# Two mixtures of experts in a decoder: finding the slots by matrix products, and moving rows per expert

## The reference

```python
gates = softmax(xt @ wg);  expert_idx = argmax(gates)       # 8 experts, one choice
mask1 = one_hot(expert_idx, E);  locations = cumsum(mask1, axis=0) - 1.0
pos = sum(locations * mask1, axis=1);  keep = pos < C        # C = 256 slots per expert
gate_val = sum(gates * mask1, axis=1) * keep
disp = zeros((E * C, M)).at[slot].add(xt * keep)             # rows into slots
h = relu(disp @ w1 + b1);  eo = h @ w2 + b2                  # 256x256x1024 and back
out = eo.reshape(E * C, M)[slot] * gate_val                  # rows back to tokens
```

## Time and profile before

| | us |
|---|---|
| median of 3 runs | 3053.37 (3043.42 to 3053.48) |
| the profiled execution | 3040.47 |
| its span | 3038.7 |
| `l0f`: norm's first operation to the next stage's | 509.7 to 769.0 |
| `l1f`: the same | 1241.4 to 1476.6 |

### The profile page before, as it was taken

One profiled execution on the slowest core, in us unless ns is written; L12 is line 12 of the kernel. 1 busy time (PEld: TensorE's weight loads), 2 busy tenths in 40 slices (PEclk: granted clock), 3 DMA queues, 4 the chain that ended last, 5 costly groups with the idle time before them and its releaser, 6 DMA issues. The chain is left out here.

```text
span 3038.7 us, 29221 instructions
## 1 busy us (share of the span) xinstructions
PE 2160.4 (71%) x10186; PEld 1346.8 (44%) x10217; DVE 1790.3 (59%) x2564; ACT 1185.1 (39%) x1864; POOL 602.7 (20%) x354
## 2 busy tenths in 40 slices
PE   3788898193599979579274888888589766074694
PEld 2455566182223337457122444444446532062374
DVE  4554455222777755511477989898545656945775
ACT  1334222010266644101135988989332224321240
POOL 2321121404142110010401545544002100000100
PEclk8899799596799999789596999999789878577896
DMA  6562100244555200044210000000210000000001
GB/s 151 87 88 25 53 1 1 90 146 85 93 84 69 29 19 1 18 142 137 54 42 14 1 1 1 1 1 1 78 31 1 32 0 0 0 7 0 19 1 34
DMA packets 104551, 124.06 MB, mean 41 GB/s; under 512 B 15824, under 2 KB 95025, under 8 KB 103382
## 3 DMA queue, kind: packets, MB, share of 16 engines
q1 hardware_dynamic: 80820, 95.99, 14.7%
q10 hardware_dynamic: 18978, 16.37, 1.7%
q0 software_dynamic: 4608, 9.85, 1.4%
HBM read 91.11 MB, written 33.03 MB: 41 GB/s over the span
## 5 line engine op out<-in xcount | busy, mean ns | idle before, releaser
L2747 DVE TENSOR_TENSOR_SCAN l2s_h<-l2s_aw 128x2048 f32<-128x2048 f32 x64 | 283.6, 4431 | 3.6 <-PE l2s_c_ps L2696 3.6
L2704 PE MATMUL l2s_big<-g_xn,g_ident 128*128 128x512 f32 x512 | 265.9, 623 | 11.7 <-ACT g_xn L2780 5.8
L2761 POOL TENSOR_SCALAR l2s_aw<-l2s_aw 128x2048 f32<-128x2048 f32 x64 | 241.2, 3769 | 152.0 <-DVE l2s_aw L2739 147.0
L568 DVE TENSOR_REDUCE l1at_nm<-l1at_s 128x1 f32<-128x512 f32 x256 | 162.2, 685 | 66.9 <-PE l1at_s L418 66.1
L2696 PE MATMUL l2s_c_ps<-g_ident,l2s_h 128*128 128x128 f32 x1024 | 156.2, 288 | 45.3 <-ACT g_xn L2780 25.4
L2696 PEld LDWEIGHTS l2s_c_ps<-g_ident,l2s_h 128*128 128x128 f32 x1024 | 123.2, 147 | 141.2 <-issue 99.7
L2780 ACT ACTIVATE g_xn<-l2s_c_ps,l2sfr_ct 128x512 f32<-128x512 f32 x256 | 165.8, 710 | 34.9 <-PE l2s_c_ps L2696 32.9
L666 ACT ACTIVATE g_xn<-l1at_s 128x512 f32<-128x512 f32 x256 | 143.4, 598 | 83.2 <-PE l1at_s L442 82.7
L2739 DVE TENSOR_TENSOR l2s_aw<-l2s_dtu,l2s_b_ps 128x2048 f32<-128x2048 f32 x64 | 146.3, 2288 | 26.8 <-remote 21.2
L2773 ACT ACTIVATE l2s_aw<-l2s_dt,l2s_A 128x2048 f32<-128x2048 f32 x64 | 129.5, 2025 | 0.0
L568 DVE TENSOR_REDUCE l0at_nm<-l0at_s 128x2 f32<-128x384 f32 x128 | 70.0, 557 | 99.6 <-PE l0at_s L418 98.7
(11 more groups left out here) (874 smaller groups left out, 4973.1 us busy)
## 6 DMA issues: line engine op xcount, KB each, us to landing
l1f_w<-in_L_ffn_w_dram SPq DMA_DIRECT2D x16, 1024.0 KB, 8.2
l0f_w<-L_ffn_experts_inter_dram SPq DMA_DIRECT2D x7, 1024.0 KB, 5.3
l0f_w<-n_L_ffn_experts_out_dram SPq DMA_DIRECT2D x7, 1024.0 KB, 8.5
l0at_qs<-l0at_parts SPq DMA_DIRECT2D x18, 256.0 KB, 9.2
l0at_ks<-l0at_parts SPq DMA_DIRECT2D x18, 256.0 KB, 19.5
l1at_qs<-l1at_parts SPq DMA_DIRECT2D x18, 256.0 KB, 8.9
l1at_ks<-l1at_parts SPq DMA_DIRECT2D x18, 256.0 KB, 19.6
l2s_gate<-l2s_aw SPq DMA_DIRECT2D x4, 1024.0 KB, 3.9
```

The source lines that it names most:

```text
L568: V.tensor_reduce(nm[:, s % 2, qts[0]:qts[-1] + 1, r], s1[:, u % 3, 0:len(qts) * KEYS].rearrange("p (q k) -> p q k", k=KEYS), AX, ALU.max, ...
L2704: nc.tensor.matmul(acc[:, tb, :], ident[:], hCT[:, tb, :], start=n == 0, stop=n == NST - 1).then_inc(acc_done, 1)
L2747: V.tensor_tensor_scan(out=h_all[:, i % 2].rearrange("p c t -> p (c t)"), data0=dA[:, i % 2].rearrange("p c t -> p (c t)"), data1=wd[:, i ...
L2761: nc.gpsimd.tensor_scalar(wd[:, i % 3], wd[:, i % 3], 10.0, -10.0, ALU.min, ALU.max).then_inc(clipped, 1)
```

## The change

The routing of a mixture becomes one block with the norm. The gate products are interleaved with the turning of `xn`; ACT alone keeps the turned tiles. The count runs in bf16, as one chain of 16 products that also adds up the tiles. The slots are found per expert instead of per token: DVE makes for each tile a 0/1 matrix `hits` (token x slot number, 128x256 bf16, L1903), PE multiplies it with `marks` (per token and expert: row number, tile number, 1, and whether it is the second choice), and the sum over the tiles gives, for each expert and slot, which token belongs in it (`take_i`) and where the result goes (`put_i`); an empty slot takes row 0 and puts out of range. SP stores `xn` plainly to the DRAM tensor `rows` during the routing, and issues the first two experts' weights ahead of it.

In the expert block POOL gathers the rows of an expert by two indirect transfers (`take`) and returns its result by two (`put_back`), to `expert_rows`, which now holds one row per token and choice. After the last return SP loads these rows plainly, four tiles at a time, and DVE adds them to `x`. The eighth expert's additions of `l0f` stand three at a time inside the first experts. The experts are written out instead of looping. At the program's start two tensors of 4096 and 2048 rows are filled with zeros, where two of 1792 and 2048 rows were.

```diff
+                    weights(sp, 0)
+                    weights(sp, 1)
+                    rows = xn_dram.rearrange("(t p) d -> p t d", p=P)
+                    for q in range(4):
+                        sp.wait_ge(xn_made, 4 * q + 4)
+                        sp.dma_start(rows[:, 4 * q:4 * q + 4, :], xn[:, 4 * q:4 * q + 4, :]).then_inc(xn_stored, 16)
+                    sp.wait_ge(xn_stored, 64)
...
+                    def turn(g):
+                        pe.wait_ge(xn_made, 2 * g + 2)
+                        if g >= 4:
+                            pe.wait_ge(tr_kept, g - 3)
...
+                        ins.then_inc(tr_ready, 1)
...
+                    def gates(g):
+                        pe.wait_ge(tr_kept, g + 1)
...
+                        for v in range(2):
+                            t = 2 * g + v
+                            for k in range(KC):
+                                ins = nc.tensor.matmul(lg_ps[:, t * NE:(t + 1) * NE], turned[:, g, (2 * k + v) * P:(2 * k + v + 1) * P], wg[:, k, :],
+                                                       start=k == 0, stop=k == KC - 1)
+                        ins.then_inc(lg_ready, 1)
+
+                    turn(0)
+                    for g in range(TILES // 2):
+                        if g + 1 < TILES // 2:
+                            turn(g + 1)
+                        gates(g)
+                    pe.wait_ge(made, MADE)
+                    pe.wait_ge(mask_ready, 1)
+                    nc.tensor.matmul(pos_ps[:, 0:TILES * NE], before_b[:], mask[:].rearrange("p t e -> p (t e)"), start=True, stop=False, skip_group_check=True)
+                    for t in range(TILES - 1):
+                        n = TILES - 1 - t
+                        ins = nc.tensor.matmul(pos_ps[:, (t + 1) * NE:TILES * NE], ones_b[:], mask[:, t, None, :].to_broadcast([P, n, NE]),
+                                               start=False, stop=t == TILES - 2, skip_group_check=True)
+                    ins.then_inc(pos_ready, 1)
...
+                    for j in range(choices):
+                        pe.wait_ge(marks_a, j + 1)
+                        pe.wait_ge(marks_d, j + 1)
+                        for t in range(TILES):
+                            pe.wait_ge(hit_made, n + 1)
+                            ins = nc.tensor.matmul(f_ps[0:PARTS * NE, 0:cap], marks[j][:, t].rearrange("p q e -> p (q e)"), hits[:, j, t, :],
+                                                   start=n == 0, stop=n == choices * TILES - 1)
+                            n += 1
+                    ins.then_inc(found_ready, 1)
+                    pe.wait_ge(found_kept, 1)
+                    for s in range(CTL):
+                        ins = nc.tensor.transpose(w_ps[:, s * PARTS * NE:(s + 1) * PARTS * NE], found[:, s * P:(s + 1) * P], ident[0:PARTS * NE, 0:PARTS * NE])
+                    ins.then_inc(index_turned, 1)
...
+                    for g in range(TILES // 2):
+                        act.wait_ge(tr_ready, g + 1)
+                        E.copy(turned[:, g, :], t_ps[:, g % 4, :]).then_inc(tr_kept, 1)
...
+                    for j in range(choices):
+                        ch.step(V.tensor_tensor(scratch[:], onehot[j][:], pos_ps[:, 0:TILES * NE].rearrange("p (t e) -> p t e", e=NE), ALU.mult))
+                        ch.step(V.tensor_reduce(place[j][:], scratch[:], AX, ALU.add))
+                        for t in range(TILES):
+                            V.tensor_scalar(hits[:, j, t, :], slot_no[:], place[j][:, t:t + 1], None, ALU.is_equal).then_inc(hit_made, 1)
...
+                    sp.wait_ge(put[u], 16 * CTL * len(range(u, n_exp, 2)))
+                for q in range(4):
+                    for j in range(choices):
+                        rows = y_dram[j * TOK:(j + 1) * TOK, :].rearrange("(t p) d -> p t d", p=P)
+                        sp.dma_start(back[:, j, 4 * q:4 * q + 4, :], rows[:, 4 * q:4 * q + 4, :]).then_inc(back_loaded[q], 16)
...
+                def take(e):
+                    u = e % 2
+                    if e >= 2:
+                        pool.wait_ge(xeT_ready, e - 1)
+                    for s in range(CTL):
+                        nc.gpsimd.indirect_dma_start(out=xe[:, u, s, :], out_offset=None, in_=xn_dram,
+                                                     in_offset=bass.IndirectOffsetOnAxis(ap=take_i[:, s, e:e + 1], axis=0),
+                                                     bounds_check=TOK - 1, oob_is_err=False).then_inc(taken[u], 16)
+
+                def put_back(e):
+                    u = e % 2
+                    pool.wait_ge(y_kept, e + 1)
+                    if e == 0:
+                        pool.wait_ge(filled, 16)
+                    for s in range(CTL):
+                        nc.gpsimd.indirect_dma_start(out=y_dram, out_offset=bass.IndirectOffsetOnAxis(ap=put_i[:, s, e:e + 1], axis=0),
+                                                     in_=ye[:, u, s, :], in_offset=None, bounds_check=choices * TOK - 1,
+                                                     oob_is_err=False).then_inc(put[u], 16)
+
+                take(0)
+                take(1)
+                for e in range(n_exp):
+                    if e + 2 < n_exp:
+                        take(e + 2)
+                    put_back(e)
+
...
+                    if l0:
+                        for t in range(3 * e, min(3 * e + 3, TILES)):
+                            ins = V.scalar_tensor_tensor(out=x[:, t, :], in0=xn[:, t, :], scalar=noop[:, t:t + 1], in1=x[:, t, :], op0=ALU.mult, op1=ALU.add)
+                            ins.then_inc(back_added, 1)
+                    dve.wait_ge(y_ready, CTL * (e + 1))
+                    if e >= 2:
+                        dve.wait_ge(put[u], 16 * CTL * (e // 2))
+                    V.tensor_copy(ye[:, u], y_ps[:, :, 0:DM]).then_inc(y_kept, 1)
+                added = TILES if l0 else 0
+                for q in range(4):
+                    dve.wait_ge(back_loaded[q], 16 * choices)
...
+                        if added:
+                            dve.wait_ge(back_added, added)
+                        for t in range(4 * q, 4 * q + 4):
+                            V.scalar_tensor_tensor(out=x[:, t, :], in0=back[:, j, t, :], scalar=weight[j][:, t:t + 1], in1=x[:, t, :],
+                                                   op0=ALU.mult, op1=ALU.add).then_inc(back_added, 1)
+                            added += 1
...
-    for n, n_exp in enumerate((7, 8)):
-        rows = n_exp * (TOK // NE)
-        disp = nc.dram_tensor(f"slots{n}", [rows, DM], F32, kind="Internal").ap()
-        eout = nc.dram_tensor(f"expert_rows{n}", [rows, DM], F32, kind="Internal").ap()
-        c[f"moe{n}"] = (disp, eout, S.sem(f"slots_zeroed{n}"))
+    for n, choices in enumerate((2, 1)):
+        rows = nc.dram_tensor(f"rows{n}", [TOK, DM], F32, kind="Internal").ap()
+        y = nc.dram_tensor(f"expert_rows{n}", [choices * TOK, DM], F32, kind="Internal").ap()
+        c[f"moe{n}"] = (rows, y, S.sem(f"rows_zeroed{n}"))
...
-                disp, _, filled = c[f"moe{n}"]
-                act.dma_start(disp.rearrange("(t p) d -> p t d", p=P),
-                              zeros[:, None, :].to_broadcast([P, disp.shape[0] // P, DM])).then_inc(filled, 16)
+                _, y, filled = c[f"moe{n}"]
+                act.dma_start(y.rearrange("(t p) d -> p t d", p=P), zeros[:, None, :].to_broadcast([P, y.shape[0] // P, DM])).then_inc(filled, 16)
```

More of the change, by code:

```diff
@@ L1694, in mixture @@
         b2_sb = None if l0 else S.sb("b2", [1, NE, DM])
-        if not l0:
-            with Scope(nc, name + "b") as B:
-                rawb = B.sb("rawb", [NE * HC, P])
-                prepare(nc, name + "bt", c, [(rawb[:], wts["b1"].rearrange("e (c p) -> (e c) p", p=P))],
-                                  [(b1_sb[:].rearrange("p e c -> p (e c)"), rawb[:])])
+        weight = [S.sb(f"weight{j}", [P, TILES]) for j in range(choices)]
+        noop = S.sb("noop", [P, TILES]) if l0 else None
@@ L1703, in mixture @@
         ye = S.sb("ye", [P, 2, CTL, DM])
-        back = S.sb("back", [P, 2, 4, DM])
-        (index_ready, scattered, loaded0, loaded1, bias_loaded, stored0, stored1, xeT_ready, xeT_copied, h_ready, h_copied,
-         y_ready, y_copied, added, step) = (S.sem(n) for n in (
-             "index_ready", "scattered", "loaded0", "loaded1", "bias_loaded", "stored0", "stored1", "xeT_ready", "xeT_copied",
-             "h_ready", "h_copied", "y_ready", "y_copied", "added", "step"))
-        loaded, stored = (loaded0, loaded1), (stored0, stored1)
@@ L1734, in _ @@
             @block.vector
             def _(dve):
-                ch = Chain(dve, step)
-                for j in range(choices):
-                    ch.step(nc.vector.tensor_scalar(back_f[:], r["slot"][j][:], float(rows - 1), None, ALU.min))
-                    ch.step(nc.vector.tensor_copy(back_i[j][:], back_f[:]))
```

(14 more changed lines are left out.)

383 lines of the change are left out of this document (232 added, 151 removed).

## The result

The changed kernel took 2943.14 us (median of 4 runs, 2938.71 to 2947.11) against 3053.43 for the kernel before, run beside it. The ratio is 0.9643, with a 95% interval of 0.9621 to 0.9665: 110 us faster. 2938 was predicted, with a range of 2912 to 2975. The profiled execution has a span of 2941.7 us; that of before had 3038.7.

A forecast was written before the change was run, and what follows sets the result against it. Bound by row traffic with PE idle (155 of the mixtures' 491.9 us), set by POOL's queue, beside products and routing. `l0f` -78.5, `l1f` -38.6, start +4 give -113.1: median 3053.4 to 2940.3; predicted 2938, range 2912 to 2975.

The forecast's parts named there:

- gate values to mask: Routing: fused operations and dropped copies save 1.15 us in `l0f` and 0.75 in `l1f`.
- the step from 2940.3 to 2938: End of the sum: median-based 2940.3 us set to 2938; one of three runs was 10 us lower.
- Products: Expert loops: no gain, 0 us, bounds -4 to +15; `y` copies 14.6 us apart in `l0f`, no PE wait for gathers.
- Turning and gate products: Routing: 32 turnings and 64 gate products, partly at full clock, save 3.5 us in each mixture.
- the never-up case: Turning and gate products with the clock never rising to full: 20.1 us, so +1.8 us.
- Mask to first rows: Routing, mask to first turned rows: 19.55 us in `l0f` (-39.0) and 15.2 in `l1f` (-22.3).
- Return: After the last `y` copy, transfers, loads and additions: 22.8 us in `l0f` (-34.9), 14.6 in `l1f` (-12.0).
- Start: Program start: 2.36 MB more zeros, 6.1 us at 385 GB/s, partly covered: +4 us, bounds 0 and +8.
- 1: Expert loops: indirect transfers hold PE 5.2 us per expert, 78 us back, 3016; chance 0.06 together with rival 4.
- 4: Row gathers: memory, not POOL, sets their cost; the scatter's 71 us stays, 3009; chance 0.06 together with rival 1.
- 2: Expert loops: clock at 0.50 instead of 0.98, +236 us, 3174, slower than before; chance 0.02.
- 3: Only half of the routing's gain: slower hits, count products and returns, half clock, zeros in full; +31, 2969; chance 0.12.

The follow-up runs named there:

- turnings first: Changed kernel with all 32 turnings before the first gate product instead of interleaved: 2933.45 us, ratio 0.9612.
- both edits: Changed kernel with all turnings before the gate products and the zero fill issued by SP at the first attention's end: 2920.28 us, ratio 0.9567.
- separated transfers: Changed kernel with all gathers before the first turned rows and all returns behind the last `ye` copy: 3006.64 us, ratio 0.9850.

## Why the prediction was right

The time was forecast at 2938 and came at 2943.1. The forecast's sum was -113.1; the medians differ by 110.3. By the two first profiles the difference is only 97.0, because that of before was a low one; with its second profile it is 107.5. The terms, from the profiles (first of each kernel):

| step | forecast | measured |
|---|---|---|
| norm's begin to gate values, `l0f`, `l1f` | -3.5, -3.5 | +1.8, +0.6 |
| gate values to mask | -1.15, -0.75 | -1.1, -0.7 |
| mask to first turned rows | -39.0, -22.3 | -41.6, -24.4 |
| expert loops | 0, 0 | -0.5, -0.4 |
| return | -34.9, -12.0 | -33.0, -11.7 |
| start | +4 | +6.8 |
| other stages | 0 | +7.3 |

Without the other stages the measured terms come to -104. They miss the forecast by 9 us, after errors that partly cancel: turning and gate products cost 9.4 more than forecast, the start 2.8, the return 2.2; the way from the mask to the rows cost 4.7 less and the loops 0.9. That the medians came out closer than that is luck: the other stages vary by several us. So was the step from 2940.3 to 2938, which rested on one low run.

**Products (right).** `ye` copies are 14.6 us apart and PE waits for no row, even at twice the transfers.

**Turning and gate products (wrong).** The step that failed is "the clock rose at about 523, after 5 us of turnings", read once and carried over to another order: in the interleaved one the clock did not rise at all. The forecast had the never-up case, +1.8, as its bound, and exactly this came in `l0f`; in `l1f` it is +0.6, since the kernel before took 27.9 us there. Undoing the interleaving alone gave it back: -5.8 and -5.6. Nor is 5 us a fixed thing. Where the turnings stand together and nothing is put ahead of them (two profiles of the kernel before, one of turnings first, one of both edits), the rise comes 2.8 to 6.0 us after the first of them.

**Mask to first rows (right, 2.6 and 2.1 us shorter than forecast).** The 16 count products took 1.3 us to DVE's next step (551.76), not 2.6; the hits 0.20 instead of 0.22; from the last index step to POOL's first transfer were 1.1 us, not 1.7. On the page of the Trainium skill that the forecast weighed: the difference of the two types is as it states, 0.07; but taken off the forecast's 0.22, as there, it gives 0.15, and 0.20 was measured. That row has two scalars and an f32 output; a comparison read from f32 took 0.27, so type alone does not explain 0.33.

**Return (right, 1.9 and 0.3 us less gained).** From the end of the last `ye` copy to the end of the last addition were 24.6 and 15.5 us against a forecast 22.8 and 14.6. In `l0f` the loads are issued 4.5 us after that end (4.4), the first addition comes 5.4 behind (4.75), and the additions took 14.7 us, at 0.43 each instead of 0.40 (13.6).

**Start (sign right, path wrong, 2.8 too small).** The step that failed is "`x` shares the engines and may come no later". By it 6.1 us of bytes became 4, and `x` came 6.8 us later. ACT could not leave its block until it had issued the fill, 8.58 us against 2.23 before, and SP's loads of `x` stand behind that block's end. The order on ACT's queue was not at work. The bytes were: the DMA engines were full until 27, and the 6.8 us are close to the undiscounted 6.1. Both delays are of one size here, so how much of the 6.8 each alone would make is not shown; the run with the loads moved shows that, with the bytes unchanged, the order alone moves `x` by 11.6. Nor is `x` "held little" beside the zeros: from its first issue to the weights that follow it were 14.7 us (2.15 to 16.89), and 9.0 without them (3.05 to 12.00). Moving only those loads gained 12.0 us in time, 6.3 of them before `l0f`; moving the fill 16.2.

**Rivals.** 1 and 4 fall by the doubled and the separated transfers. 2 (slower) did not come: the clock in the loops is 0.98 and 0.97. Of 3, half clock throughout came true, and most of the start (6.8 of 8); the hits at 0.33 and the count products at 0.22 did not.

The +7.3 in other stages need not be the change's doing: against the second profile of before the same stages are 2.3 us shorter, not longer (the attention and cross attention before `l0f` 488.2 to 486.6, the stretch between the mixtures 479.3 to 477.7, all behind `l1f` 1564.6 to 1565.5). That stretch was 472.5 and 479.3 us for the kernel before and 473.9 to 481.2 with the edits. Its low phases of the clock fall differently; what places them stays open.

## What to carry to other kernels

Indirect transfers of 128 rows of 1 KB cost their queue's beat here, 1.30 us each, where their bytes at 385 GB/s would be 0.34. Put them beside products: four per expert (5.2 of 14.6 us) and even eight (10.4) cost the products nothing. Transfers of other sizes were not run, so what the beat follows, rows or bytes, stays open. When a short chain of products is re-ordered, look at the granted clock and not at PE's busy share; here 32 turnings of 128 columns in a row raised it, and the same 32 among products of 8 columns did not. Before a fill or another large transfer goes first "since nothing waits for it", look who stands behind the issuing engine's block, since a busy issue is a wait for everyone at the block's end, and count its bytes in full if something that is waited for comes beside it.

## What was not expected of the hardware

- Issuing blocks. The fill of 6144 rows of 1 KB kept ACT for 8.58 us, beside the loads of `x` for 13.88, and one weight load behind it 6.11 us instead of 0.47. Why an issue takes so long is not tested.
- The clock stayed at 0.50 for 20 us of uninterrupted PE records when groups of four turnings alternated with 8-column products.
- Full clock came for 3 to 7 us for the same instructions, and a stage of unchanged instructions, in which the clock's low phases fall differently, took 472.5 to 481.2 us.
- Additions of 128x256 f32 ran 0.43 us apart with one wait per eight, 0.47 with one per four; the forecast had taken 0.40 from the earlier trace rows.
